# Two transformer layers in one kernel: query and key stacks with three heads side by side, and the row maxima sent through memory

## The reference

```python
qkv = jnp.einsum('bld,ed->ble', x, W_qkv)
qkv = qkv.reshape(b, 3, H, L, D_H)
Q, K, V = (qkv[:, 0], qkv[:, 1], qkv[:, 2])
scores = jnp.einsum('bhqd,bhkd->bhqk', Q, K) * D_H ** (-0.5)
attn = jax.nn.softmax(scores, axis=-1)
out = jnp.einsum('bhqk,bhkd->bhqd', attn, V)
out = out.transpose(0, 2, 1, 3).reshape(b, L, D_IN)
```

## Time and profile before

| | before |
|---|---|
| median of 3 runs | 906.05 us |
| profiled execution | 901.82 us |
| its span | 898.6 us |
| mean granted TensorE clock | 0.886 of full |
| PE busy | 700.2 us (78%) |
| DVE busy | 597.0 us (66%) |
| ACT busy | 449.5 us (50%) |
| POOL busy | 410.0 us (46%) |
| DMA packets | 298,170, of which 237,352 under 512 B |
| DMA share of 16 engines, main queue | 54.2% |

### The profile page before, as it was taken

The page is one execution under the profiler, slowest core; times in us unless marked ns, Lnnn a source line. Parts: engine busy times, 40 slices in busy tenths (PEclk is TensorE's granted clock), DMA queues, the critical chain, the costliest instruction groups (busy, mean ns, idle before and its releaser), DMA issues.

```text
span 898.6 us, 14775 instructions
## 1 busy us (share of the span) xinstructions
PE 700.2 (78%) x5100; PEld 552.5 (61%) x5100; DVE 597.0 (66%) x1429; ACT 449.5 (50%) x897; POOL 410.0 (46%) x601
## 2 busy tenths in 40 slices
...
GB/s 180 59 0 13 66 76 67 75 68 75 69 86 77 79 68 86 67 88 53 101 53 103 52 103 59 96 48 108 36 118 37 106 36 107 37 106 3 12 12 12
DMA packets 298170, 60.57 MB, mean 67 GB/s; under 512 B 237352, under 2 KB 293616, under 8 KB 298096
## 3 DMA queue, kind: packets, MB, share of 16 engines
q1 hardware_dynamic: 298096, 59.63, 54.2%
...
## 4 chain that ended last, share of the span: by engine, by line
PE 30%; DMA 23%; DVE 19%; SPq 12%; issue 8%; POOL 4%; ACT 2%; POOLq 0%; DVEq 0%; ACTq 0%
DMA qk_scratch<-qk_part 13%; DMA kT<-qk_scratch 9%; SPq L418 7%; PE pA L590 7%; PE pB L606 6%; DVE nmax L1236 5%; SPq L446 4%; PE pC L707 4%; PE pO L658 3%; PE pS L632 2%; PE pA L529 2%; DVE spec L1080 2%; PE pC L729 1%; POOL hid_lo L1445 1%; PE pS L682 1%
## 5 line engine op out<-in xcount | busy, mean ns | idle before, releaser
L1236 DVE TENSOR_REDUCE nmax<-pB 128x2 f32<-128x512 f32 x256 | 167.9, 678 | 87.5 <-PE pB L606 86.5
L862 ACT ACTIVATE pt<-pS 128x512 f32<-128x512 f32 x256 | 149.1, 602 | 75.0 <-PE pS L632 74.0
L606 PE MATMUL pB<-kT,qT 96*128 96x256 bf16 x512 | 104.0, 306 | 51.5 <-DMA kT<-qk_scratch 48.0
L632 PE MATMUL pS<-qT,kT 98*128 98x256 bf16 x512 | 97.0, 294 | 25.7 <-DMA qT<-nmaxT 20.0
L1422 POOL TENSOR_TENSOR hsum<-hsum,hsq 128x512 f32<-128x512 f32 x48 | 63.5, 1322 | 95.8 <-ACT hsq L902 95.8
L606 PEld LDWEIGHTS pB<-kT,qT 96*128 96x128 bf16 x512 | 42.4, 107 | 87.3 <-DMA kT<-qk_scratch 52.5
L1417 POOL TENSOR_TENSOR hh<-hr 128x512 f32<-128x512 f32 x64 | 68.4, 1069 | 40.7 <-ACT hr L890 40.7
L707 PE MATMUL pC<-x3T,w1T 128*128 128x256 f32 x256 | 81.4, 343 | 5.0 <-ACT hr L890 2.7
L1445 POOL TENSOR_TENSOR hid_lo<-hh,hid 128x512 fp32r<-128x512 f32 x64 | 81.8, 1278 | 1.3
L632 PEld LDWEIGHTS pS<-qT,kT 98*128 98x128 bf16 x512 | 45.2, 105 | 58.9 <-DMA qT<-nmaxT 21.0
L707 PE MATMUL pC<-x3T_lo,w1T 128*128 128x256 f32 x256 | 74.0, 315 | 0.0
...
## 6 DMA issues: line engine op xcount, KB each, us to landing
...
```

The source lines that it names most:

```text
L606: ins = pe.matmul(pB[h % 2][:, s * T:(s + 1) * T], qT[k][0:STACK, u * P:(u + 1) * P], kT[k][0:STACK, h * T:(h + 1) * T], start=True, stop= ...
L632: ins = pe.matmul(pS[h % 2][:, s * T:(s + 1) * T], kT[k][:, u * P:(u + 1) * P], qT[k][:, h * T:(h + 1) * T], start=True, stop=True)
L862: act.activation(pt[:, (h // 4) % 2, h % 4].rearrange("p s n -> p (s n)"), pS[h % 2][:], ACT.Exp, scale=HD ** -0.5).then_inc(S["probs"], 1)
L1236: dve.tensor_reduce(nmax[:, h * SIDES:(h + 1) * SIDES], pB[h % 2][:].rearrange("p (s k) -> p s k", s=SIDES), AX.X, ALU.max, negate=True).t ...
```

## The change

Queries and keys are held in `qk` as two sides, two windows of positions, and within a window three heads (`SLOTS`) side by side at each position: six rows of windows and thirds, 18 slots for 16 heads. One piece of a `g_out` is now 2 x 16 x 3 bf16 = 192 B (before 64 B), one piece of a `g_in` 256 x 3 bf16 = 1.5 KB (before 512 B), and the bytes are 18/16 of before. The matmuls of b_max and e_score read columns three elements apart, for both operands. Each g_qkv_sb becomes five copies (four of 96 columns for queries and keys, one of 192 for values). qk_scratch becomes a double buffer, and the waits on it loosen. The maxima are no longer transposed: `b_spread` writes them from `nmax_s` to memory in pieces of three bf16, and `b_rows` reads two rows back. `ORDER` is new on all engines; what stands at the seam of a turn is also noted differently there.

The core of the diff:

```diff
-    "g_out_1:+1 w_load:+1 w_load_fc:+1 b_rows:+1 g_in_0:+1 g_out_2:+1 w_load_proj:+1 g_in_1:+1 g_in_2:+1 "
-    "p_load c_store:+1 g_v_in:+1 g_out_0 g_v_out "
+    "g_v_out:+2 g_out_1:+2 c_store:+3 b_rows:+2 g_in_0:+2 w_load_fc:+2 g_out_2:+2 p_load:+1 "
+    "w_load_proj:+2 w_load:+1 g_in_1:+2 g_in_2:+2 g_v_in:+2 g_out_0:+1 b_spread:+1 "
...
+THIRDS, WINS, SLOTS = 3, 2, 3
+FIRST_K, FIRST_V = 5, 10
+RUN = 2 * HD * SLOTS
...
-        qT = [sb(f"qT{k}", [STACK + 2, UNITS * P], BF16) for k in range(2)]
-        kT = [sb(f"kT{k}", [STACK + 2, UNITS * P], BF16) for k in range(2)]
+        qT = [sb(f"qT{k}", [STACK + 2, WINS * THIRDS, T, SLOTS], BF16) for k in range(2)]
+        kT = [sb(f"kT{k}", [STACK + 2, WINS * THIRDS, T, SLOTS], BF16) for k in range(2)]
...
-                sp.dma_start(scratch[n].rearrange("(u p n) -> p u n", p=P, n=2 * HD),
-                             flat2(qk_part[n]).rearrange("p (u n) -> p u n", n=2 * HD)).then_inc(S[PART_OUT[n]], 16)
+                sp.dma_start(scratch[k, n].rearrange("(x p n) -> p x n", p=P, n=RUN),
+                             qk_part[n][:].rearrange("p w r n -> p (w r) n")).then_inc(S[PART_OUT[n]], 16)
...
-                            sp.dma_start(dst[r * HD:(r + 1) * HD, :].rearrange("d (h n) -> d h n", h=HEADS),
-                                         scratch[n].rearrange("(w h d n) -> w d h n", w=2, h=HEADS, d=HD)[w]
+                            sp.dma_start(dst[r * HD:(r + 1) * HD].rearrange("d r n a -> d r (n a)"),
+                                         scratch[k, n].rearrange("(w r d n) -> w d r n", w=2, r=WINS * THIRDS, d=HD)[w]
                                          ).then_inc(S["qk_in"], 16)
...
+            def b_spread(i, k):
+                sp.wait_ge(S["maxt_split"], nth(i, PER["maxt_split"], 1))
+                apart(sp)
+                if has(i, 2):
+                    sp.wait_ge(S["max_in"], before(i, PER["max_in"], back=2))
+                apart(sp)
+                sp.dma_start(max_scratch[k].rearrange("(x p a) -> p x a", p=P, a=SLOTS),
+                             nmax_s[:].rearrange("p t r s a -> p (t r s) a")).then_inc(S["max_out"], 16)
+
             def b_rows(i, k):
-                sp.wait_ge(S["maxt_sb"], nth(i, PER["maxt_sb"], 1))
+                sp.wait_ge(S["max_out"], nth(i, PER["max_out"], 16))
                 apart(sp)
                 if has(i, 2):
                     sp.wait_ge(S["score_ready"], before(i, PER["score_ready"], back=2))
                 apart(sp)
-                for t in range(2):
-                    sp.dma_start(qT[k][STACK + t:STACK + t + 1, :], nmaxT[UNITS * t:UNITS * (t + 1), :]
-                                 ).then_inc(S["max_in"], 16)
+                sp.dma_start(qT[k][STACK:STACK + 2].rearrange("t r n a -> t (r n a)"),
+                             max_scratch[k].rearrange("(t n) -> t n", t=2)).then_inc(S["max_in"], 16)
...
                 for s in range(SIDES):
-                    u = h * SIDES + s
-                    ins = pe.matmul(pB[h % 2][:, s * T:(s + 1) * T], qT[k][0:STACK, u * P:(u + 1) * P],
-                                    kT[k][0:STACK, h * T:(h + 1) * T], start=True, stop=True)
+                    ins = pe.matmul(pB[h % 2][:, s * T:(s + 1) * T], query(qT[k], h)[0:STACK, s * P:(s + 1) * P],
+                                    key(kT[k], h)[0:STACK], start=True, stop=True)
...
+                for w in range(2):
+                    for o in range(WINS):
+                        first = FIRST_K * w + SLOTS * o
+                        act.copy(qk[:, w, o, n:n + 3 * (HD - 1) + 1:3], bank[:, first:first + SLOTS]
+                                 .rearrange("p a b h -> p b h a")).then_inc(S["qk_sb"], 1)
+                if n == 0:
+                    if has(i):
                         act.wait_ge(S["v_out"], before(i, PER["v_out"]))
-                act.copy(qkv[:, n:n + 3 * (T - 1) + 1:3, :], pA[1][:].rearrange("p (h n) -> p n h", h=2)
-                         ).then_inc(S["qkv_sb"], 1)
+                act.copy(vals[:, :, n:n + 3 * (HD - 1) + 1:3], bank[:, FIRST_V:]).then_inc(S["v_sb"], 1)
...
+        def query(v, h):
+
+            o, a = divmod(h // THIRDS, SLOTS)
+            return v[:, THIRDS * o + h % THIRDS, :, a]
```

More of the change, by code:

```diff
@@ L98 @@
 ORDER = (
[4 rows of a table removed]
[L104 removed]
[14 rows of a table removed]
[L121 to L122 removed]
[6 rows of a table removed]
[5 rows of a table added]
+    "b_max_14 a_prt b_max_15 e_ont a_attn c_ms e_wo e_vt:-1 c_y g_x1t:-1 "
[15 rows of a table added]
+    "a_bn w_sign_1_1:+1 g_low "
[4 rows of a table added]
 ).split()
 PER = dict(
[L136 removed]
+    x_in=16, v_out=16, v_in=16, hi_out=16, mid_out=16, low_out=16, qk_in=192, max_out=16, max_in=16, y_out=16,
     xt_ready=1, proj_ready=2, proj_sb=2, cum_ready=1, cum_even=1, prt_ready=1, attn_ready=1, x1t_ready=1, gate_ready=1,
     mixt_ready=1, ffn_ready=1, x2t_ready=1, qkv_ready=3,
[L139 removed]
+    xt_sb=1, squares=1, prt_sb=1, x1t_sb=1, x1_sq=2, gate_exp=1, mixt_sb=1, x2t_sb=1, qk_sb=12, v_sb=3, first_done=1, rest_done=1, mid_done=1, low_done=1, vt_ready=1, v_ready=1,
     norm_ss=2, crossed=3, root_step=14, norm_rs=1, spectra=2, products=2, a_pow=1, a_var=2, a_moments=2, a_eps=1, g_pow=1, g_var=2, g_moments=2, g_eps=1, x1_done=2, gate_arg=1, mix_done=1,
@@ L217, in mega_kernel @@
         mix = sb("mix", [P, SIDES, P])
-        mixT = sb("mixT", [P, SIDES, P])
         two_less = sb("two_less", [P, SIDES])
         x2 = sb("x2", [P, SIDES, D])
-        qk_part = [sb(f"qk_part{n}", [P, 2 * ROWS, 2], BF16) for n in range(3)]
-        qkv = sb("qkv", [P, 3 * ROWS, 2])
+        qk_part = [sb(f"qk_part{n}", [P, 2, WINS * THIRDS, RUN], BF16) for n in range(3)]
+        qk = sb("qk", [P, 2, WINS, THIRDS * HD, 2, SLOTS])
+        vals = sb("vals", [P, HD - FIRST_V, THIRDS * HD, 2])
         v_heads = sb("v_heads", [P, 2, T])
@@ L281, in mega_kernel @@
         pO = bank("pO")
-        pBb = [b[:, :].bitcast(BF16) for b in pB]
         S = {n: ctx.enter_context(nc.semaphore(n)) for n in PER}
@@ L301, in mega_kernel @@
         ones_ready = ctx.enter_context(nc.semaphore("ones_ready"))
+        max_zeros = ctx.enter_context(nc.semaphore("max_zeros"))
         pool_const = ctx.enter_context(nc.semaphore("pool_const"))
@@ L394, in g_out @@
                     apart(sp)
-                    if has(i):
-                        sp.wait_ge(S["qk_in"], before(i, PER["qk_in"]))
+                    if has(i, 2):
+                        sp.wait_ge(S["qk_in"], before(i, PER["qk_in"], back=2))
                     apart(sp)
@@ L452, in c_store @@
                 sp.dma_start(out[i].rearrange("(p s) d -> p s d", s=SIDES), y[:]).then_inc(S["y_out"], 16)
-            steps = dict(p_load=p_load, g_v_out=g_v_out, g_v_in=g_v_in, b_rows=b_rows, c_store=c_store,
+            steps = dict(p_load=p_load, g_v_out=g_v_out, g_v_in=g_v_in, b_spread=b_spread, b_rows=b_rows, c_store=c_store,
                          w_load=w_load, w_load_fc=w_load_fc, w_load_proj=w_load_proj)
```

97 lines of the change are left out of this document (47 added, 50 removed), and 44 rows, old and new, of the table ORDER.

## The result

The changed kernel takes 1088.8 us (median of 4 runs, 1082.4 to 1097.9), the kernel before 905.8 (902.1 to 907.2): ratio 1.204, 95% interval 1.194 to 1.213. It is slower, as forecast, but the time lies far above the forecast (965) and its range (860 to 1000). The profiled span is 1088.5 us at a mean granted clock of 0.84.

What follows compares the result with a forecast made beforehand. A loop through several engines and the stack transfers bounds the turn. Transfers +0.8, b_max_0 to g_out_0 +2.7, clock +0.6: 4.1 us over 15 turns, 61; with prologue, last turn and median, 967, rounded to 965; range 860 to 1000.

Steps and rivals of the forecast that it cites:

- The bound: Each turn is a loop from T0 (start of b_max_0) to F (issue of g_out_0) and through transfers to T0.
- g_in: Stack transfers in: 16 partitions limit them, larger pieces gain nothing; 13.1 us where 11.7 stood, +1.4 a turn.
- Rival 1: Piece size was the limit of g_in: at 185 GB/s or more the kernel gets faster, down to 855 us; 22%.
- g_out: Stack transfers out: 192 B pieces take 1.8 us for 2.4, three times a turn, -1.7.
- the closed gap of 2.5: Empty DMA engines while SP issues b_rows; other transfers would now fill that time: -2.5 us a turn.
- b_spread: Write of the maxima: 3072 pieces of 6 B take 1.8 us, bounds 0.9 and 5.4, landing about 6 us after g_out_0's issue.
- e_score_0: Its 1.6 us wait for the maxima's rows stays or grows to 3.4, absorbed at b_max_0; last turn +1.
- The stride: Matmuls of b_max and e_score reading columns three apart cost nothing; twice the time would be +3.5 us a turn.
- The order: Steps moved behind b_max_0's start on PE and DVE; with evacuation +2.7 us up to g_out_0's issue, bounds 1.5 and 4.5.
- the split evacuation: On ACT the last g_qkv_sb becomes five copies for one: 1.1 to 1.4 us for 0.63, taken as +0.7.
- The clock: PE idles longer before b_max_0, so its granted clock is low more often: +0.6 us a turn.
- slower still: 6-byte pieces at three times the price or strided operands at twice the time: 1015 us; 8%.

Runs made afterwards that it cites:

- a5: The changed kernel with g_in_0 issued ahead of b_rows on SP; 1127.4 us, ratio 1.249 to the kernel before.
- m1_micro: The kernel before, with groups of matmuls and single transfers timed behind its last instruction; ran once; 0.172 us a matmul with moving operand three apart, 0.109 side by side.
- a3: a2 with the ORDER of the kernel before, b_spread between g_out_0 and g_v_out; scores wrong; 846.8 us, ratio 0.937.
- a1: The changed kernel, but b_spread writes one piece of 144 B per partition, 128 pieces instead of 3072; 963.0 us, ratio 1.063 to the kernel before.
- b2: The kernel before plus a write of 3072 adjacent 6 B pieces after g_out_0, for which b_rows waits; 1061.5 us, ratio 1.179.
- a2: a1 with b_max and e_score reading adjacent columns instead of columns three apart; scores wrong; 908 us, ratio 1.002 to the kernel before.
- b1: The kernel before with b_max and e_score reading columns three elements apart; scores wrong; 919.2 us, ratio 1.021.
- a4: a2 with two scores, g_mix and e_out_1 back ahead of b_max_0 on PE, and g_res2, g_bn, g_mean ahead of DVE's reads; 877.2 us, ratio 0.972.

## Why the prediction was right and wrong

**The bound: right.** The turn is still the loop T0, F, T0, and it ends at the stack transfers, with PE's own path from e_score_0 close behind (a5).

**g_in: right.** No gain from 1.5 KB pieces: in the turn shown its two halves of 0.88 MB move in 6.8 and 7.3 us, 131 and 121 GB/s, for 135 in the sum. From the issue of b_rows to the last kT it was 17.1 us (564.94 to 582.08), and the terms of the sum for it are 0.3 + 6.5 + 1.8 + 0.8 + 6.6 + 1.2 = 17.2. Rival 1 is dead: m1_micro has 94 and 99 GB/s for the two sizes.

**g_out: right, a little small.** 1.6 us of transfer for 2.4, where the sum had 1.8 (a3). Against the kernel before, F to T0 is 3.4 us shorter in a3 (22.8 for 26.2 in the mean). Three g_outs at 0.8 less and the closed gap of 2.5, less the 1.4 for the bytes of g_in, come to 3.5 (an estimate from these terms). F to T0 without small pieces is 22.7, 22.4 and 22.8 us in the means of a1 to a3, under the 24.4 that my sum gives without its 1.8 for b_spread. One term of the difference can be named: the 1.6 us for c_store and p_load ahead of g_in_2. In a3 they stand behind it again, and the stretch is no shorter, though the two orders differ in more than that.

**b_spread: the step that failed.** I priced it by its pieces, 9.4 ns each since a piece of 64 B costs that the earlier trace rows, 1.8 us in all with 5.4 as the upper bound, and had it land about F+6. The price of moving a piece held (9.6 ns in m1_micro); that a DMA has landed soon after its last piece did not. It lands 12.5 to 14.0 us after its issue, F+14.4 in the turn shown. Nothing in the trace of before said what happens when ten pieces share 64 B, and "three times" was no bound, only a guess. The second half of the step failed too: "v_out, out_1 and the store still run then" was to cover it, but they stand in the same queue and were themselves held up: 12.1 us of issuing for 3.3, g_v_out's 2048 pieces moving for 9.8 us in the turn shown where a1 has 2.0, and v_scratch landing after 13.7 us. Cover on the same queue was no cover. F to T0 grew by 8.3 us in the mean (31.05 against 22.74 in a1) for the 1.8 of the sum. Price: 126 us of the 183 (a1), 160 in the kernel before (b2).

**e_score_0.** I let its wait grow to 3.4 us at most and had b_max_0 absorb it. It is 9.3 us in the turn shown, and a5 shows that the 12.4 us of PE work from there to b_max_0 make it a second path of nearly equal length. Behind the last T0 the wait for the rows stands alone: +1 forecast, +13.7 measured, of which +3.4 is left without the small pieces (a1).

**The stride: taken as nothing, 55 us.** The other miss. I took this term as nothing, without a row for it. It is 0.172 us for 0.109 a matmul; twice was my bound (+3.5 a turn). Between T0 and F stand 22 pairs, 22 x 0.126 = 2.8 us. T0 to F shrank by 3.7 in the mean from a1 to a2 (4.4 between the turns shown); the rest fits two DVE operations that came to lie beside POOL's work on 128x512 elements (`hh`, `hid_lo`). DVE's groups in the changed kernel (busy us, mean ns):

```profile
L1101 DVE TENSOR_TENSOR spec<-raw_spec,rn 128x512 f32<-128x512 f32 x32 | 43.6, 1402 | 0.0
L1062 DVE TENSOR_SCALAR x<-x,mvg,rsg 128x256 f32<-128x256 f32 x32 | 35.5, 1150 | 1.3 <-POOL rsg L1382 1.3
```

The same two take 1430 and 1112 ns in a1, 989 and 568 in a2, 818 and 456 in the kernel before: 2.0 us a turn between a1 and a2. Of the 32 TENSOR_SCALARs, 26 stand beside those operations of POOL in a1 and take 0.98 to 1.36 us each; in a2 it is 5, and the others take 0.4 to 0.5. That this is why 55 us went and not 18 (b1) fits these rows; it is not shown by a run of its own. The Trainium skill (SBUF — State Buffer, the note on cachelines under "Door 1: The DMA port swizzle") lets bf16 stride up to 8 elements for free; the runs contradict it from 3 on, and at 4 the matmul takes twice as long. The Trainium skill (SBUF — State Buffer, "SBUF: two separate sides") has DVE and GpSimd (POOL) share a port pair that one of them holds for a whole instruction, when DVE reads two inputs from SBUF or runs in a two-port mode; the lengths of the two DVE operations go with that, but no run here shows the port.

**The order: right in kind, small.** +2.7 was forecast for T0 to F from the moved steps and the split evacuation. a2 against a3 measures +4.2 in the mean (22.8 against 18.6), and the steps I named are half of the time (a4). The evacuation, which a3 keeps, cost nothing there: 18.6 us, for 19.2 before. So the 0.7 for it was hidden, and the order without a named culprit cost more.

**The clock.** +0.6 was forecast. After the long wait g_mix takes 1.89 us in the turn shown, where the row of before has 1.03; its four matmuls and the output products after them run at a granted clock of 0.50. A second such stretch is new: the clock is at 0.50 from 562.6 to 572.9 as well, around the 9.3 us in which PE waits for the rows. The mean clock fell from 0.886 to 0.84. a1 has 0.887 again, so this share is inside its 126 us; how large it is was not taken apart.

**The range.** 8% went to "slower still", with 1015 as its time. Its two causes were the two that happened; the first was sized by what stood nearest, and it cost 8.3 us a turn for 1.8, over the bound of 5.4. The sign was right with some luck: a2, which has neither cause, takes 908 us, as long as the kernel before, where the sum without its 1.8 us a turn for b_spread comes to 938 (965 - 27, an estimate from its own terms). The other terms alone did not make it slower.
